# Cross-attention of a decoder layer: statistics and normalisation of the next batch's inputs moved into the last two steps of the batch in front

## What is computed

```python
xn = layer_norm(ctx, g1, b1)              # context tokens
ln_lat = layer_norm(x, g2, b2)            # x: output of the self-attention
q = ln_lat @ Wq
k, v = split(concatenate([xn, ln_lat], axis=1) @ Wkv)   # 512 keys, 16 heads of 64
weight = softmax(where(mask, q @ k.T / 8, -max))
x = layernorm(x + (weight @ v) @ Wout)
```

## Time and profile before

| what | us |
|---|---|
| median of 3 runs | 2677.26 (2676.36 to 2679.8) |
| profiled execution, its time | 2674.3 |
| profiled execution, its span | 2672.5 |
| PE busy in the span | 2363.7 |
| DVE busy | 1866.2 |
| ACT busy | 1760.6 |
| POOL busy | 1033.2 |

### The profile page before, as it was taken

How to read it: one execution, slowest core, us unless ns; L and a number is a source line. 1 busy time by engine, 2 the same in 40 slices (tenths; PEclk the granted TensorE clock), 3 DMA queues, 4 the chain that set the end, 5 groups by cost and what they waited for, 6 DMA issues and landing times. The chain is left out here.

```text
span 2672.5 us, 62026 instructions
## 1 busy us (share of the span) xinstructions
PE 2363.7 (88%) x18020; PEld 1960.6 (73%) x18020; DVE 1866.2 (70%) x5239; ACT 1760.6 (66%) x4480; POOL 1033.2 (39%) x1112
## 2 busy tenths in 40 slices
PE   5888888886799999999999999999999379999991
PEld 4676777674577777777777777777776279999990
DVE  5666766666577766876677666776686368788776
ACT  4888888885466666666566666766576256676662
POOL 3453444444443333333333334333332134444434
PEclk8999999999899999999999999999999689999995
DMA  4645554453100000000000000000000166777765
GB/s 126 175 109 116 126 130 107 111 120 80 33 10 16 17 17 1 16 17 17 3 15 16 17 9 8 16 17 17 1 16 9 65 221 226 242 235 229 240 220 197
DMA packets 160230, 224.40 MB, mean 84 GB/s; under 512 B 33873, under 2 KB 127697, under 8 KB 159569
## 3 DMA queue, kind: packets, MB, share of 16 engines
q1 hardware_dynamic: 149040, 201.88, 26.9%
q0 software_dynamic: 9664, 20.53, 2.3%
q10 hardware_dynamic: 1376, 0.54, 0.1%
HBM read 140.15 MB, written 24.01 MB: 61 GB/s over the span
## 5 line engine op out<-in xcount | busy, mean ns | idle before, releaser
L1358 ACT COPY x_pt<-x_ptb 128x512 f32<-128x512 f32 x512 | 272.2, 583 | 193.6 <-PE x_ptb L1800 192.9
L1553 DVE CUSTOM_DVE_ANT_0 wox<-x_score,x_mask_add 128x512 f32<-128x512 f32 x352 | 239.3, 683 | 166.5 <-PE x_score L1788 115.3
L1352 ACT ACTIVATE wox<-wox,x_low 128x512 f32<-128x512 f32 x352 | 251.8, 718 | 100.8 <-DVE x_low L1553 97.4
L1254 POOL TENSOR_TENSOR x_k_lo<-x_whole,x_k_hi 128x512 fp32r<-128x512 f32 x128 | 164.5, 1285 | 336.8 <-ACT x_k_hi L1399 335.1
L484 ACT ACTIVATE prob<-prob,low 128x128 f32<-128x128 f32 (+1 forms) x512 | 233.7, 468 | 55.3 <-DVE low L727 54.0
L1817 PE MATMUL x_av<-x_pt,x_vx 128*64 128x256 f32 x2048 | 249.3, 385 | 0.6 <-ACT x_ox_hi L1366 0.6
L1532 DVE COPY x_whole<-x_proj 128x512 f32<-128x512 f32 x192 | 130.6, 686 | 128.4 <-PE x_proj L1718 127.1
L1564 DVE TENSOR_SCALAR wox<-wox,x_rden 128x512 f32<-128x512 f32 x352 | 201.9, 615 | 0.6
L2217 ACT ACTIVATE h_t<-h_bank,b_s 128x256 f32<-128x256 f32 x312 | 130.8, 470 | 107.2 <-PE h_bank L2436 99.7
L2436 PE MATMUL h_bank<-xg_hi,w_hi 128*128 128x256 f32 x624 | 177.9, 285 | 22.1 <-DVE xg_lo L2309 20.7
L1817 PEld LDWEIGHTS x_av<-x_pt,x_vx 128*64 128x64 f32 x2048 | 135.5, 136 | 80.8 <-issue 11.8
(11 more groups left out here) (296 smaller groups left out, 8080.0 us busy)
## 6 DMA issues: line engine op xcount, KB each, us to landing
w_s<-w SPq DMA_DIRECT2D x156, 512.0 KB, 4.9
k_parts<-k_hi SPq DMA_DIRECT2D x128, 128.0 KB, 2.4
q_parts<-q_hi SPq DMA_DIRECT2D x128, 128.0 KB, 2.4
k_parts<-pos_parts SPq DMA_DIRECT2D x128, 64.0 KB, 2.4
k_parts<-k_lo SPq DMA_DIRECT2D x64, 128.0 KB, 2.4
q_parts<-q_lo SPq DMA_DIRECT2D x64, 128.0 KB, 2.4
w_s<-expert_rows SPq DMA_DIRECT2D x16, 512.0 KB, 5.0
b_s<-b SPq DMA_DIRECT2D x39, 128.0 KB, 3.0
```

Of the source, the lines that this page charges most:

```text
L1254: pool.tensor_tensor(part_of(n, q_lo, k_lo), whole_of(n), part_of(n, q_hi, k_hi).bitcast(F32), ALU.subtract).then_inc(low_ready.sem, 1)
L1352: nc.scalar.activation(slot, slot, ACT.Exp, bias=low[:, u:u + 1], scale=-1.0, accum_out=den[:, u:u + 1]).then_inc(exp_ready.sem, 1)
L1358: nc.scalar.copy(pt[:, u % PX_RING, :], ptb[u % 2][:, :]).then_inc(pt_taken[u % 2].sem, 1)
L1553: dve.tensor_tensor_reduce(prob_slot(u), score[u % 2][:, :], mask_add[:, :], -X_SCALE, 3.0e38, ALU.add, ALU.min, low[:, u:u + 1]).then_inc ...
```

## The change

The statistics move from step 1 to step 18 of the pass in front, the normalisation from step 2 to step 19 of the pass in front, and POOL's two `reciprocal_root` of the inputs from the head of its pass to the end of the pass in front, behind `low_ox(b, 7)`. The first pass's inputs are now handled ahead of the loops. The last loop pass handles a batch that does not exist (its load was made before too).

```diff
+            for ln in (LN_LAT, LN_CTX):
+                reciprocal_root(0, ln)
             ox_over = {1: 2, 3: 3, 6: 4, 8: 5, 10: 6, 11: 7}
             with pool.Fori(0, B - 1) as b:
                 lows_over(b, 0)
-                for ln in LNS:
-                    reciprocal_root(b, ln)
+                reciprocal_root(b, LN_X2)
                 low_keys(b)
...
+                for ln in (LN_LAT, LN_CTX):
+                    reciprocal_root(b + 1, ln)
                 list_extended(b)
...
-                    if not isinstance(b, int):
+                    if not (isinstance(b, int) and b < 0):
                         dve.wait_ge(keys_split.sem, keys_split.at(b - 1, n + 1))
...
-            steps = {0: [last_values], 1: [v_part(V1, 1, 1), input_stats], 2: [input_normalised], 3: [residual_sum], 4: [v_part(V1, 3, 1), x2_of],
+            steps = {0: [last_values], 1: [v_part(V1, 1, 1)], 3: [residual_sum], 4: [v_part(V1, 3, 1), x2_of],
...
-                     17: [part(11)]}
+                     17: [part(11)], 18: [lambda b: input_stats(b + 1)], 19: [lambda b: input_normalised(b + 1)]}
...
+            input_stats(0)
+            input_normalised(0)
             dve.wait_ge(weights_split, N_WEIGHTS + 1)
             with dve.Fori(0, B - 1) as b:
                 one_pass(b, steps)
```

## The result

The changed kernel takes 2839.84 us (median of 6 runs, 2831.66 to 2843.47) against 2678.16 before (6 runs): ratio 1.0598, 95% interval 1.0581 to 1.0614. Slower by 162 us; forecast was 138. The profiled execution has a span of 2838.1 us, 165.6 more than before.

What follows compares the result with a forecast made beforehand. PE was taken to bound a pass, except DVE in steps 2 to 4. From 2674.3 us, stalls of 137.8 less 20.6 gain plus 21 clock gave 2812.5 profiled, 2816 as median (+5.2%); range 2776 to 2846.

Steps and rivals of the forecast that it cites:

- gain in steps 2 to 4, a pass: Cross-attention steps 2 to 4: PE waits less for DVE once statistics and normalisation leave; 1.37 us a pass, 20.6 overall.
- wait for POOL, `rstd` of the context behind the last `low_ox`: At a pass's end POOL makes rstd behind low_ox(b, 7), which ends at 1151.91; the context's is ready at 1153.98.
- over the seam: Between two passes, from the start of DVE's last instruction to its first unit of the next: 3.6 us.
- PE's stall, 14 seams: In front of the scores of step 1, PE stands still 9.2 us at each of 14 pass boundaries.
- clock, a pass: Behind each seam's stall PE restarts at a lowered clock; 1.4 us a seam, bounds 0 and 3.4, 21 us overall.
- the last seam: At the fifteenth seam DVE runs on into the written-out last pass, and PE waits about 6.3 us.
- ahead of the first pass: Before the first pass, two POOL roots, normalisation and waits delay DVE's first unit by 2.7 us.
- The wait of 0.18 us: Sign: PE's 0.18 us wait for DVE's low in front of scores, in steps 2 to 4, would be gone.
- the slices of the clock row: Sign: through the cross-attention, slices of the profile's clock row would stand at 0.8 to 0.9.
- the hidden restart: Rival: at the seam DVE's loop restart of 2.8 us hides in its wait for rstd; 2777 us, chance 0.08.
- The rival on the other side: Moved work fits DVE's idle time before the seam, only gain stays: 2657 us; 2685 with roots at once; chance 0.03.

Runs made afterwards that it cites:

- e1: Changed kernel with POOL's two input roots moved earlier, right behind the tenth low_part instead of behind low_ox(b, 7); 2722.46 us.
- e2: Kernel before, nothing moved, with one wait added in DVE's step 19 for the pass's last low_ox; 2814.56 us.
- e3: Changed kernel with the normalisation left in step 2; statistics in step 18 and POOL's roots at the pass's end; 2661.25 us.
- e4: On e1: statistics moved to step 17 in front of part(11), normalisation to step 18; 2664.41 us.
- e6: On e3: statistics moved from step 18 to step 17 in front of part(11), normalisation still in step 2; 2657.18 us.
- e7: Changed kernel with SP's two input loads put behind its wait for x2_ready instead of in front of it; 2818.59 us.
- e5: Changed kernel with 70 unused matmuls added on PE in front of the scores of step 1, filling its idle time; 2812.66 us.

## Why the prediction was right, and where its terms were off

The direction, the mechanism and the place were right: POOL's queue order makes `rstd` the last thing of a pass, DVE waits for it 7.2 us (forecast about 7), and PE's scores of step 1 come 9.5 to 9.9 us late. e1 shows that the order in POOL's queue is the cause, e2 that the wait is enough without the moved work, e3, e4 and e6 that the moved work without the wait is a gain. Term by term:

| term, us | forecast | measured |
|---|---|---|
| gain in steps 2 to 4, a pass | 1.37 | 1.44 (86.61 - 85.17) |
| wait for POOL, `rstd` of the context behind the last `low_ox` | 2.07 | 2.1 (1298.66 to 1300.77) |
| over the seam | 3.6 | 4.0 to 4.4; 3.2 in e7 |
| PE's stall, 14 seams | 9.2 | 9.72 |
| clock, a pass | 1.4 (0 to 3.4) | 2.4 |
| the last seam | 6.3 | 5.84 |
| ahead of the first pass | 2.7 | 2.4 of 7.6 |

The 24 us by which the median was missed are the stall (14 x 0.5 = 7 us), the clock (14 x 1.0 = 14 us) and 3 us net of the small terms and of the start of the phase, which no step of the change explains.

The step that failed is one that was costed at nothing: "The two loads of SP are released at the seam instead of in step 2, behind no other wait, and are wanted a pass later: nothing." The loads are indeed not wanted until later, but where they run now they meet DVE's restart, and the term of 3.6 us for the seam became 4.2. e7 puts their price at 21 us, 14 of stall and the rest through the clock. The question was not who waits for the transfer but what the transfer is in the way of. Without this collision the same sum, with e7's 3.2 us for the seam, would give 2816 - 14 x 0.4 = about 2810 us, and with e7's 1.7 us of clock about 2815; e7 takes 2818.59.

The clock term was mis-sized, inside its bounds. It was argued from one stretch of 3.4 us at 0.51, which followed a wait of 1.55 us. In the changed kernel the clock is down from 1299.3, long before PE resumes at 1306.64, and comes back at 1313.0, 6.4 us later.

The gain's size is right in part by luck. The sum gave 0.58 us of it to the statistics and 0.79 to the normalisation, but e6 has all of it with the normalisation left in step 2. With the statistics gone, PE's waits there are the same in the changed kernel and in e6 (0.67 and 0.17 us). What went is 0.58 us, 0.26 of the 0.93, and a wait for ACT that the prediction did not count. It stands in the timeline of PE before, and in the loop of no kernel without statistics in step 1:

```profile
1160.90 1.09 PE L1800 MATMUL x_ptb<-ident,wox 128*128 128x128 f32 x8 [0.46 <-ACT x_pt L1358]
```

Two of the signs named in advance did not show. The wait of 0.18 us did not go (0.17), and the slices of the clock row from 780 to 2130 us all stay at 9: the clock is down for 10 to 14 us of a pass's 97, which leaves a mean of 0.94 (window from 2080 to 2177).

Of the rivals, the hidden restart fell: "issue" in front of the first unit grew from 2.82 to 3.64 us, though DVE had waited 7.21 us for POOL just before. With it falls, for this engine and this body, the figure of about 108 ns for a branch (the Trainium skill, "Advanced Engine Details and Errata", Control Flow Timing): DVE takes at least 3.4 us from its branch to its first unit. The Trainium skill, "Runtime: NRT & Kernel Launch", Instruction fetch mechanics, says that a taken branch to a place outside the fetch window has to fetch it before execution goes on. The trace agrees for this loop, by the instruction queue's transfers 1.0 to 2.3 us behind the branch, which are absent at the fifteenth seam, where the loop is left, and by e7.

The rival on the other side fell too. e1, with the roots early, still has PE 2.5 to 3.1 us late, where the prediction had 1.9, and takes 2722 us, not 2685. Its second context instruction starts 5.4 us behind the start of the copy, not 4.1, because of the slower pair and 0.7 us of waits for POOL. With the 3.3 us that its restart takes, PE's wait is 2.77 us on average, which makes 12 us over the passes. Another 89.30 - 85.17 - 2.77 = 1.4 us a pass (19 us) are the clock, which that estimate had left out.

What stood open behind e3, why the restart takes 3.5 to 3.8 us before, 3.4 to 3.7 in e3 and 3.2 in e7, is a matter of where one starts to count. From DVE's branch the three take the same 3.4 to 3.8 us. The branch runs 0.09 us behind the start of the last instruction (the copy) before, 0.02 us behind it in e3, and 0.2 us ahead of it in e7. What stays open is what the 3.4 us themselves consist of.

## What to carry to other kernels

Before filling idle time in front of a loop's end, check that the inputs of the work are ready there: look at what stands last in the queue of the engine that serves it. Here POOL's in-order queue turned a helper of 1 us into the end of the pass. The 2.4 us of statistics fitted and won 0.7% (e3, e6); with 1.3 us of normalisation behind a late root the kernel lost 6%. When a step is moved, ask of each transfer that it releases not only who wants it but what else runs at the new time, a loop's instruction fetch included. And a stall of PE cost more than its length here: 9.7 us of idling took 2.4 more through the clock, 8.8 us took 1.7 (e7), and 6.5 us took 2.5 (e2). The longer stall is not always the dearer one.

## What the runs showed of the hardware that was not expected

- DVE's loop of the cross-attention takes 3.4 to 3.8 us from its branch to its next instruction at every turn, although DVE was idle for 3.9 us shortly before; ACT's loop in the same phase takes 0.2 us. Loads of 256 KB issued from 0.2 us ahead of the branch make DVE's 4.0 to 4.7 us; issued 1.0 us behind it they make no difference (e4).
- Filling PE's idle time with useless matmuls (e5) made the changed kernel 27 us faster: the clock stayed at 2.4 GHz.
- A pair of DVE's tensor_scalar over 128x256 took 2.02 us instead of 0.73 in every pass in which it met a tensor_tensor of POOL over 128x512 (e1); that this is the cause was not tested.
